# Edge pass of a graph layer: TensorE posts its semaphores from a drain instead of from a matmul

## The reference

```
xn   = layernorm(x)
h    = xn @ W.T                                   # 8 heads of 32
enc  = relu(edge_attr @ edge_W.T + edge_b)        # per edge
alpha= h[src].a_src + h[dst].a_dst + sum(enc * h[dst])
attn = softmax over the edges of one dst (leaky relu first)
gnn  = segment_sum(h[src] * attn, dst)
x    = x + gnn + mix(xn)                          # linear attention and a feed forward
x    = x + ffn(layernorm(x))                      # 8 experts, one chosen per token
```

## Time and profile before

| | |
|---|---|
| median of 3 runs | 5232.41 us |
| lowest run | 5230.8 us |
| span of the profiled execution | 5158.3 us |
| lowest run less that span | 72.5 us |
| TensorE busy (matmuls) | 3767.6 us, 73% |
| VectorE / ScalarE / POOL busy | 2599.5 / 2112.2 / 2005.2 us |
| edge pass, stretch of nearly all its items | 1060 to 4292 us of the span |

### The profile page before, as it was taken

One profiled execution on the slowest core, in us unless ns is written; L12 is line 12 of the kernel. 1 busy time (PEld: TensorE's weight loads), 2 busy tenths in 40 slices (PEclk: granted clock), 3 DMA queues, 4 the chain that ended last, 5 costly groups with the idle time before them and its releaser, 6 DMA issues.

```text
span 5158.3 us, 88906 instructions
## 1 busy us (share of the span) xinstructions
PE 3767.6 (73%) x22054; PEld 2527.9 (49%) x22055; DVE 2599.5 (50%) x6056; ACT 2112.2 (41%) x5703; POOL 2005.2 (39%) x2172
## 2 busy tenths in 40 slices
PE   4788997677677667677767667777766667891999
PEld 3357886344444444444434444444444444771888
DVE  5556554455555555555555555555555555440111
ACT  3212332344444444444444444444444445442332
POOL 3120000555455544455544555555554442005111
PEclk8889998788888888888888888888888888895999
DMA  4610111333333333333333333443333332102110
GB/s 151 225 44 17 34 33 49 92 99 100 97 97 101 99 99 99 97 100 100 102 100 94 101 100 99 105 102 98 102 102 100 100 101 93 72 22 59 36 36 28
DMA packets 352302, 449.27 MB, mean 87 GB/s; under 512 B 170970, under 2 KB 275163, under 8 KB 350456
## 3 DMA queue, kind: packets, MB, share of 16 engines
q0 software_dynamic: 95568, 267.78, 19.8%
q10 hardware_dynamic: 108050, 122.83, 7.8%
q1 hardware_dynamic: 148231, 53.53, 4.3%
HBM read 389.57 MB, written 55.13 MB: 86 GB/s over the span
## 4 chain that ended last, share of the span: by engine, by line
PE 39%; another core or an unknown queue 17%; issue 15%; DVE 12%; ACT 6%; ACTq 6%; DMA 3%; DVEq 1%; POOL 1%; SPq 0%; POOLq 0%
PE bank L1099 6%; PE bank L1040 5%; PE bank L1183 4%; PE bank L1195 4%; PE bank L1143 3%; PE bank L1005 3%; PE bank L1014 3%; ACT dist L770 3%; DVE prod L1460 3%; PE bank L1061 2%; ACTq L355 2%; DVE msg L1540 2%; ACTq L737 2%; PE bank L1030 2%
## 5 line engine op out<-in xcount | busy, mean ns | idle before, releaser
L514 POOL DMA_INDIRECT al<-h_tab,idx x976 | 975.4, 999 | 1021.5 <-issue 970.8
L752 ACT ACTIVATE enc<-bank,eb 128x512 f32<-128x512 f32 x880 | 555.3, 682 | 1601.5 <-remote 1338.1
L514 POOL DMA_INDIRECT gbuf<-h_tab,idx x784 | 786.5, 1003 | 821.3 <-issue 738.5
L1061 PE MATMUL bank<-prod,hsel 128*32 128x128 f32 x7040 | 336.9, 317 | 928.5 <-issue 779.0
L1040 PE MATMUL bank<-oneh_t,hbt 125*128 125x512 bf16 x2640 | 839.4, 464 | 38.0 <-issue 33.9
L1061 PEld LDWEIGHTS bank<-prod,hsel 128*32 128x32 f32 x7040 | 199.4, 122 | 1098.5 <-issue 916.4
L1460 DVE SCALAR_TENSOR_TENSOR prod<-enc,adst,bank 128x512 f32<-128x512 f32 x880 | 629.1, 736 | 25.8 <-remote 10.9
L1099 PE MATMUL bank<-msg,oneh 128*125 128x264 f32 x2352 | 613.1, 406 | 14.9 <-DVE r L1549 9.1
L1549 DVE TENSOR_TENSOR r<-r,bank 125x264 f32 x440 | 188.5, 428 | 757.8 <-remote 534.3
L1099 PEld LDWEIGHTS bank<-msg,oneh 128*125 128x125 f32 x2352 | 476.8, 204 | 154.4 <-issue 45.9
L770 ACT ACTIVATE dist<-iota_n,dtile 128x125 f32<-128x125 f32 x1760 | 551.1, 384 | 2.0 <-issue 0.5
(11 more groups left out here) (255 smaller groups left out, 5399.6 us busy)
## 6 DMA issues: line engine op xcount, KB each, us to landing
dstb<-dst ACTq DMA_DIRECT2D x440, 125.0 KB
al<-pen_d SPq DMA_DIRECT2D x1760, 4.0 KB
att<-attrx ACTq DMA_DIRECT2D x880, 24.0 KB
al<-h_tab,idx POOLq DMA_INDIRECT x976
link<-links SPq DMA_DIRECT2D x880, 0.2 KB
gbuf<-h_tab,idx POOLq DMA_INDIRECT x784
attrx<-al ACTq DMA_DIRECT2D x8, 1176.0 KB, 12.3
hsplit<-hb POOLq DMA_DIRECT2D x25, 375.0 KB, 5.2
```

What stands on the lines that cost most here:

```text
L514: pool.indirect_dma_start(slot(n)[:, c, :], None, h_tab, bass.IndirectOffsetOnAxis(ap=idx[g % 2][:, k:k + 1], axis=0)).then_inc(gathered[n ...
L752: m = act.activation(enc[n % 2][:, k, :], bank[k][:, :], ACT.Relu, bias=eb[:, k:k + 1])
L1061: m = pe.matmul(bank[7][32 * c:32 * c + 32, 0:128], hsel[:, i, :], prod[n % 2][:, k, c * 128:(c + 1) * 128], start=(i == 0 and k == 0), st ...
```

## The change

In the edge pass no matmul carries an increment any more. Behind the last matmul of each piece stands a `drain` on TensorE, and the drain carries the increment. Of each item there are four (`enc_mm`, `d_ready`, `r_ready`, `m_used`), of each group three more (`ends_up`, `ends_down`, `ex_turned`). Which engine waits for what, and for which value, stays as it is, but that the value awaited of `node_in` is computed from `t & 63` instead of `t`, which gives the same number, since `t` is at most 49.

```
-                    act.wait_ge(node_in, t * 16)
+                    act.wait_ge(node_in, (t & 63) * 16)
...
# e_enc
-                m.then_inc(enc_mm, 1)
+                pe.drain().then_inc(enc_mm, 1)
...
# e_dst
-                pe.wait_ge(node_in, t * 16 + 16)
+                pe.wait_ge(node_in, (t & 63) * 16 + 16)
...
-                m.then_inc(d_ready, 1)
+                pe.drain().then_inc(d_ready, 1)
...
# e_sum
-                m.then_inc(r_ready, 1)
+                pe.drain().then_inc(r_ready, 1)
...
# g_up
-                pe.matmul(bank[7][0:33, A0:A0 + 128], ends[1], ident[:, ::-1], ...).then_inc(ends_up, 1)
+                pe.matmul(bank[7][0:33, A0:A0 + 128], ends[1], ident[:, ::-1], ...)
+                pe.drain().then_inc(ends_up, 1)
...
# g_down
-                m.then_inc(ends_down, 1)
+                pe.drain().then_inc(ends_down, 1)
...
# g_turn
-                pe.matmul(bank[7][:, A1:A1 + 128], exr[:, :], ident[:, :], ...).then_inc(ex_turned, 1)
+                pe.matmul(bank[7][:, A1:A1 + 128], exr[:, :], ident[:, :], ...)
+                pe.drain().then_inc(ex_turned, 1)
...
# m_sum
-                m.then_inc(m_used, 1)
+                pe.drain().then_inc(m_used, 1)
```

More of the change, by code:

```diff
@@ L1029, in e_enc @@
                 for k in range(KC):
-                    m = pe.matmul(bank[k][:, :], ew_bf[32 * k:32 * k + 24, k * 128:(k + 1) * 128], att[b][32 * k:32 * k + 24, :], start=True, stop=True)
-                m.then_inc(enc_mm, 1)
+                    pe.matmul(bank[k][:, :], ew_bf[32 * k:32 * k + 24, k * 128:(k + 1) * 128], att[b][32 * k:32 * k + 24, :], start=True, stop=True)
+                pe.drain().then_inc(enc_mm, 1)
             def e_dst(n, t):
@@ L1039, in e_dst @@
                     for a in range(3):
-                        m = pe.matmul(bank[2 + 2 * q + k][:, :], hbt[:, ds(t & (HT - 1), 1), a, k * 128:(k + 1) * 128].rearrange("p t c -> p (t c)"), oneh_t[q][:, :], start=(a == 0), stop=(a == 2))
-                m.then_inc(d_ready, 1)
+                        pe.matmul(bank[2 + 2 * q + k][:, :], hbt[:, ds(t & (HT - 1), 1), a, k * 128:(k + 1) * 128].rearrange("p t c -> p (t c)"), oneh_t[q][:, :], start=(a == 0), stop=(a == 2))
+                pe.drain().then_inc(d_ready, 1)
             def bank7_read(k):
@@ L1060, in e_sum @@
                     for c in range(4):
-                        m = pe.matmul(bank[7][32 * c:32 * c + 32, 0:128], hsel[:, i, :], prod[n % 2][:, k, c * 128:(c + 1) * 128], start=(i == 0 and k == 0), stop=False, skip_group_check=True)
+                        pe.matmul(bank[7][32 * c:32 * c + 32, 0:128], hsel[:, i, :], prod[n % 2][:, k, c * 128:(c + 1) * 128], start=(i == 0 and k == 0), stop=False, skip_group_check=True)
                 if i == G - 1:
                     pe.wait_ge(asrc_kept, n + 1)
-                    m = pe.matmul(bank[7][:, 0:128], apad[(n // G) % 2], ident[:, :], start=False, stop=True, skip_group_check=True)
-                m.then_inc(r_ready, 1)
+                    pe.matmul(bank[7][:, 0:128], apad[(n // G) % 2], ident[:, :], start=False, stop=True, skip_group_check=True)
+                pe.drain().then_inc(r_ready, 1)
             def new_sums():
@@ L1074, in g_up @@
                 pe.matmul(bank[7][0:33, A0:A0 + 128], ends[0], ident[:, :], start=False, stop=False, skip_group_check=True)
-                pe.matmul(bank[7][0:33, A0:A0 + 128], ends[1], ident[:, ::-1], start=False, stop=False, skip_group_check=True).then_inc(ends_up, 1)
+                pe.matmul(bank[7][0:33, A0:A0 + 128], ends[1], ident[:, ::-1], start=False, stop=False, skip_group_check=True)
+                pe.drain().then_inc(ends_up, 1)
             def g_down(g):
@@ L1081, in g_down @@
                     pe.wait_ge(oneh_ready, G * (g - 1) + 1)
-                    m = pe.matmul(bank[7][0:P, B2:B2 + H], oneh[(G * (g - 1)) % NM][0:1, 0, :], dl[0:1, 1, :], start=False, stop=False, skip_group_check=True)
+                    pe.matmul(bank[7][0:P, B2:B2 + H], oneh[(G * (g - 1)) % NM][0:1, 0, :], dl[0:1, 1, :], start=False, stop=False, skip_group_check=True)
                 if g < NG:
                     pe.wait_ge(links_made, g + 1)
-                    m = pe.matmul(bank[7][:, B0:B0 + 2], fin[:, :], ident[0:33, 0:33:32], start=False, stop=False, skip_group_check=True)
-                m.then_inc(ends_down, 1)
+                    pe.matmul(bank[7][:, B0:B0 + 2], fin[:, :], ident[0:33, 0:33:32], start=False, stop=False, skip_group_check=True)
+                pe.drain().then_inc(ends_down, 1)
             def g_turn(g):
@@ L1091, in g_turn @@
                 pe.matmul(bank[7][0:1, B1:B1 + H], smax[:, 0:1], ident[:, 0:H], start=False, stop=False, skip_group_check=True)
-                pe.matmul(bank[7][:, A1:A1 + 128], exr[:, :], ident[:, :], start=False, stop=False, skip_group_check=True).then_inc(ex_turned, 1)
+                pe.matmul(bank[7][:, A1:A1 + 128], exr[:, :], ident[:, :], start=False, stop=False, skip_group_check=True)
+                pe.drain().then_inc(ex_turned, 1)
             def m_sum(n):
@@ L1098, in m_sum @@
                 for c in range(4):
-                    m = pe.matmul(bank[6][0:P, 0:HO], oneh[n % NM][:, c, :], msg[n % NM][:, c, :], start=(c == 0), stop=(c == 3))
-                m.then_inc(m_used, 1)
+                    pe.matmul(bank[6][0:P, 0:HO], oneh[n % NM][:, c, :], msg[n % NM][:, c, :], start=(c == 0), stop=(c == 3))
+                pe.drain().then_inc(m_used, 1)
             def group_at(k, lag):
```

## The result

The changed kernel takes 5784.86 us (median of 4 runs, 5775.67 to 5822.07) against 5247.18 us for the kernel before (4 runs, 5230.8 to 5269.83): **1.104 times as long**, 95% interval 1.099 to 1.109. The profiled execution took 5775.67 us with a span of 5773.8 us. The forecast was 5860 us and slower.

What follows compares the result with a forecast made beforehand. The edge pass was taken to be paced by TensorE's posts, late while gathers run. 5.3 + 1.8 + 2.2 = 9.3 us an item, 1.44 above 7.86, gave 634 us more over 440 items: 5860 us predicted, range 4800 to 6250.

Steps and rivals of the forecast that it cites:

- The mechanism's first half: Edge pass, TensorE: a drain waits for matmul completions held while gathers run; slower, chance 0.52, 5860 us.
- The reading behind it: TensorE's held posts come out together and in order, so what stands is a queue of matmul completions.
- the drains' own price: Edge pass: lost overlap, drain ends and restarts, sequencer work and group drains add 1.8 us an item, bounds 1.0 to 3.0.
- The base: TensorE's step without holds: 4.63 us with posts on time, plus 0.7 for low-clock steps, 5.3 us an item.
- Lost overlap: TensorE can no longer run into the next piece, so piece ends stop overlapping: 0.46 us an item.
- The forecast's other terms, the gaps: Drain ends and restarts 0.56, sequencer waits and register operations 0.39, drain instructions 0.20, groups' drains 0.23 us an item.
- the forecast's own sign: Line 1061 to the next should take 6.4 us where no gather runs, if the drains' 1.8 us are right.
- The hold: Late completions under gathers now stand in TensorE's path: 0.56 of items times a mean 3.9 us, 2.2 us an item.
- The upper bound: Worst slow case, the drains' upper bound with the hold's full length: 10.2 us an item, 6260 us.
- The fast case: Rival, chance 0.38: the drain posts on time despite gathers; 7.1 us an item, 4900 us.
- The case of no change: Rival, chance 0.10: posts come on time, but drains at 2.5 us an item give it all back; 5210 us.

Runs made afterwards that it cites:

- e5: Changed kernel, but `e_sum` keeps its increment on the matmul and has no drain: 5541.88 us, 1.0696 of the kernel before.
- e1: Changed kernel with the increments back on the matmuls and a drain without a post kept behind each piece: 5705.07 us, 1.1043 of the kernel before.
- e3: Kernel before with one gather per item in place of four from item 16 on: 4230.55 us, 0.818 of the kernel before.
- e4: Changed kernel with one gather per item in place of four from item 16 on: 4825.76 us, 0.933 of the kernel before.
- e1 to e4: e1, e3, e4 and one more: kernel before with only `e_sum` posting by a drain, 5400.41 us, 1.0438 of the kernel before.
- e9: Kernel before, all four gathers, but rows of 32 bytes in place of 1088 from item 16 on: 5186.05 us, 1.0035 of the kernel before.
- the table of four runs: Shares of the kernel before: increments on matmuls 1 with four gathers, 0.818 with one (e3); drains 1.104 with four, 0.933 with one (e4).
- e10: Changed kernel with a second, bare drain ahead of each of the 2091 that post: 5889.04 us, 1.1377 of the kernel before.

## Why the prediction was right, step by step

**The direction** was right, the size somewhat high: 1.44 us an item were forecast, 1.22 measured (538/440). The 1.40 of the two profiles is nearer only because the profile before is of a faster occasion, and the 5860 us started from the median of the slower one. The mechanism's first half, that a drain waits for what is held, is shown by the 1.60 us behind line 1061 and by the 10.1 us drain of e5. The reading behind it, that the posts come out in order as a queue of completions, has more for it in the trace of the kernel before. Its records of semaphore updates have TensorE's posts 14 ns behind the modelled end of their matmul in the stages outside the pass (44 behind one line), and `enc_mm` 1.9 us behind it in the pass, both in the median, while ScalarE's posts stay at 9 to 10 ns in the pass. When the hold ends, the posts follow each other 42 ns apart where 2 matmuls lie between them, 76 with 6 and 159 with 16, within 1 ns in most cases.

**The sum was partly right by luck: its terms erred both ways.** By terms, per item, from the runs of one occasion (e1 is the changed kernel's case, and costs the same):

| term | forecast, us | measured, us |
|---|---|---|
| step without holds, no drains | 5.3 | 5.67 (e3) |
| the drains' own price | 1.8 | 1.35 (e4 less e3) |
| what gathers add with drains | 2.2 | 2.00 (e1 less e4, 879/440) |
| sum | 9.3 | 9.02 |

- **The base** left out that TensorE waits for others even without holds. In e3 it is idle for (2280 - 1976)/402.5 = 0.75 us an item.
- **The drains.** Lost overlap was priced at 0.46 us an item and is 0.44 (busy 5.35 in e4 less 4.91 in e3). The forecast's other terms, the gaps, add to 1.38 us; in the timeline of e4 the gaps are 3 x 0.23 + 0.62 + 3/4 x 0.23 = 1.48. So the price was right for a step that waits for nothing else, and the forecast's own sign shows it: a step where no gather runs should take 6.4 us, and behind the last gather of the changed kernel one takes 6.5.

```profile
4937.36 0.64 PE L1061 MATMUL bank<-prod,hsel 128*32 128x128 f32 x16 [0.23 <-issue]
...
4943.89 0.65 PE L1061 MATMUL bank<-prod,hsel 128*32 128x128 f32 x16 [0.23 <-issue]
```

What failed is that no credit was given. In e4 idle time is 1.64 us an item in all, and e3 has 0.75 of waits without any drain: in both, part of the idle time is TensorE waiting for the others. So the drains' gaps fill time in which TensorE would have waited, which the forecast put at nothing: 0.44 and 1.48 would be 1.92 us, and 1.35 are paid.
- **The hold.** Its term was taken as a wait alone. Of the 2.00 us, idle time is 2.79 - 1.64 = 1.15, and busy time is 6.21 - 5.35 = 0.86. The second part is the clock: the granted clock is 0.85 in e1 and 0.96 in e4, and pieces run at the lower of the two levels, as in the row of 2.74 us. The first part stands at `e_sum`'s drain, whose median is 1768 ns in the changed kernel against 613 in e4. The forecast put 0.7 us of clock and of waits before `fac` into the base and 2.2 of wait on top.
- **The upper bound.** 10.2 us is not the sum of its terms: 5.3 + 3.0 + 2.2 is 10.5, some 6390 us in place of 6260. The measured time is far from either.

**What the forecast did not see:** the gathers cost the kernel before just as much by late posts, 2.14 us an item (e3), as they cost the kernel with drains, 2.00. The change did not make the hold dearer; it moved it from the readers of the posts to the drains and added the drains' own price. "The drain waits for what is held" is true, and it decides the direction, since it means that nothing is won; but it is not what made the difference. e1 to e4 show that. The prediction's own sum had it so without saying it: 7.86 less its 5.3 gives the hold 2.56 us before the change, and 2.2 after it, so all that it adds is the 1.8 of the drains.

**The rivals.** The fast case was to be decided by a relu that starts within 0.2 us of line 1030's end under gathers. It does, in the row at 2511.68, and the kernel is still slower, since line 1030 itself comes late: this sign was badly chosen. The case of no change needed posts on time and 2.5 us of drains an item; the drains cost less than that and no hold went away.

The rule of the Trainium skill in "PSUM — Partial Sum Buffer", section "Engine vs sequencer instructions", is that a drain waits for the engine to go fully idle. e5 agrees in that the drain waits for the earlier pieces too; in its row of 10.1 us the engine computes nothing any more for some 9 of them, so what counts as idle there is the report of the matmuls, and not the matmuls as the profile shows them. The 26 ns an increment that the Trainium skill has in "TensorE: Matmul & The Clock Gate", section "The cost: per-tile semaphore tail", would by estimate have made e1 54 us slower than the changed kernel, 0.010. Measured is 0.001 with intervals of 0.003 and 0.005, so nothing of it shows here.

**Open:** by what way the gathers hold TensorE's completions. No experiment kept the count of gathers and took rows away from each, so which of the two counts holds them is open too. e3 and e4 take away GpSimd's work along with the gathers; e9 excludes the bytes alone. No version tried is both complete and faster than the kernel before.

## What to carry to other kernels

A post that comes late need not be the fault of who carries it: see whether the engine runs on past it. If it does, a drain puts the delay into the engine's own path. Here each of the 2091 drains cost 595/2091 = 0.28 us where hardly anything was held, so by this account it is cheapest where the engine would wait anyway; no run here moves it there. To find what a hold costs, take its cause away in both versions; the table of four runs shows whether two costs meet or only add up.

## What the runs showed of the hardware

- One gather per item in place of four took 18% off the kernel, and rows of 32 bytes in place of 1088 took nothing off: the late posts go with the number of gathers (and of the rows they fetch), not with bytes.
- A drain on an idle TensorE is shown as 13 ns and costs 70 to 84 ns (e10). One behind work leaves 0.23 us until the next matmul, 0.62 us where the sequencer's waits and register operations follow it (e4).
- A drain waits for the report that earlier matmuls are done, and while gathers run that report can come some 9 us after their modelled end (e5).
- Part of the gathers' cost comes by the clock. With four gathers the granted clock is 0.83 and TensorE is busy 5.52 us an item before and 6.35 after the change; with one gather it is 0.94 and 4.91 (e3), 0.96 and 5.35 (e4).
